# Turning 16-bit tiles: from TensorE transposes to transposing transfers in a two-layer transformer kernel

## The reference

```python
xn = _layernorm(x)
x = x + _L0_attn_ref(xn, ...) + _L0_ffn_ref(xn, w_gating, w_linear)
xn = _layernorm(x)
x = x + _L1_attn_ref(xn, ...) + _L1_ffn_ref(xn, w_gate_up, w_proj)
```

## Time and profile before

| | |
|---|---|
| time, median of 3 runs (lowest, highest) | 600.28 us (598.49, 602.88) |
| the profiled execution: its span, its own time as the profile has it | 601.7 us |
| last sum on VectorE in it | 598.4 us |
| TensorE busy | 562.0 us (93%), 5153 products |
| ScalarE busy | 469.6 us (78%) |
| VectorE busy | 426.6 us (71%) |
| GpSimd busy | 233.6 us (39%) |
| queue 1's packets, share of 16 engines | 24.4% |

### The profile page before, as it was taken

The page is one execution under the profiler, slowest core; times in us unless marked ns, Lnnn a source line. Parts: engine busy times, 40 slices in busy tenths (PEclk is TensorE's granted clock), DMA queues, the critical chain, the costliest instruction groups (busy, mean ns, idle before and its releaser), DMA issues. The chain is left out here.

```text
span 601.7 us, 13300 instructions
## 1 busy us (share of the span) xinstructions
PE 562.0 (93%) x5153; PEld 290.7 (48%) x5153; DVE 426.6 (71%) x909; ACT 469.6 (78%) x607; POOL 233.6 (39%) x302
## 2 busy tenths in 40 slices
...
GB/s 265 303 36 2 36 1 35 36 2 49 6 62 33 33 59 39 27 37 3 19 17 2 64 54 27 89 55 27 54 10 36 45 20 69 17 68 85 94 57 48
DMA packets 150914, 30.40 MB, mean 51 GB/s; under 512 B 133952, under 2 KB 149568, under 8 KB 150848
## 3 DMA queue, kind: packets, MB, share of 16 engines
q1 hardware_dynamic: 150272, 29.19, 24.4%
...
## 5 line engine op out<-in xcount | busy, mean ns | idle before, releaser
L958 ACT ACTIVATE Pt<-psS 128x1024 f32<-128x1024 f32 x288 | 281.7, 1047 | 44.8 <-PE psS L685 25.9
L699 PE MATMUL psV<-Pt,vaug 128*32 128x512 f32 x1152 | 150.3, 611 | 0.3 <-POOL Pt L1645 0.3
L1645 POOL TENSOR_SCALAR_AFFINE_SELECT Pt<-Pt 128x1024 f32<-128x1024 f32 x64 | 71.7, 1145 | 43.8 <-ACT Pt L958 43.8
L685 PE MATMUL psS<-qTf,kTf 32*128 32x512 f16 x576 | 74.9, 390 | 7.3 <-ACT Pt L958 3.7
L685 PEld LDWEIGHTS psS<-qTf,kTf 32*128 32x128 f16 x576 | 20.3, 91 | 82.9 <-ACT Pt L958 48.1
L1695 POOL TENSOR_TENSOR ss<-ss,mhalf 128x1 f32<-128x1 f32 x16 | 9.5, 596 | 111.3 <-DVE ss L1476 111.3
L699 PEld LDWEIGHTS psV<-Pt,vaug 128*32 128x32 f32 x1152 | 25.7, 109 | 41.9 <-issue 35.9
L1016 ACT ACTIVATE stage<-psS 128x1024 f32<-128x1024 f32 x32 | 31.0, 1020 | 8.1 <-PE psS L821 7.9
L1686 POOL TENSOR_TENSOR r<-qk,cos 128x256 f32<-128x256 f32 x16 | 11.9, 744 | 63.9 <-ACT qk L991 58.0
L866 PE MATMUL psB<-wguT,xhs 128*128 128x512 bf16 x108 | 27.8, 380 | 0.0
L1032 ACT ACTIVATE qtmp<-qtmp 128x1024 bf16<-128x1024 f32 x16 | 16.9, 1059 | 12.9 <-PE psA L876 8.4
...
## 6 DMA issues: line engine op xcount, KB each, us to landing
...
G<-qkvscr SPq DMA_DIRECT2D x24, 128.0 KB, 3.7
stage<-in_wg SPq DMA_DIRECT2D x4, 512.0 KB, 8.8
w8g<-qkvscr SPq DMA_DIRECT2D x16, 128.0 KB, 3.8
oscr<-o SPq DMA_DIRECT2D x16, 128.0 KB, 3.3
at<-oscr SPq DMA_DIRECT2D x16, 128.0 KB, 2.0
out<-yout SPq DMA_DIRECT2D x16, 128.0 KB, 2.5
...
```

What stands on the lines that cost most here:

```text
L685: e.matmul(psS[j], kd[32 * j:32 * j + k, h, 128 * at:128 * at + 128], qd[32 * j:32 * j + k, 4 * h:4 * h + 4, :].rearrange("p s n -> p (s n ...
L699: ins = e.matmul(psV[32 * j:32 * j + 32, :], vaug[:, at, j, 32 * h:32 * h + 32], Pt[(4 * Q + j) % NP], start=(kb == 0 and h == 0), stop=(k ...
L958: e.activation(flat(Pt4[:, u % NP:u % NP + 2, :]), flat(psS4[:, j:j + 2, :]), ACT.Exp, scale=scale).then_inc(S["exp"], 1)
L1645: e.affine_select(out=p, in_=p, pattern=[[0, 8], [1, 128]], compare_op=ALU.is_ge, fill=0.0, base=0, channel_multiplier=-1).then_inc(S["mas ...
```

## The change

Three kinds of turns of 16-bit numbers leave TensorE: qxT, the layernorm's xn1T in the first pass, and hxT. Each becomes a transfer of SyncE's queue that turns on its way, from one on-chip buffer into the other (`dma_start_transpose`): kt (2 squares a tile, 64 KB), qt (8, 256 KB), xt (4, 128 KB: the split into 16-bit halves is now made before the turn, by the new stage xs of VectorE) and ht (16, 512 KB). The copies kTc, qTc, xn1Tc and hTc go. 448 transposes of TensorE, 80 fills of the shared banks and 96 operations of VectorE go, 32 of VectorE and 64 transfers come. All other stages keep their order on every engine; the transfers are put between the older ones in SyncE's order. Readers wait for the transfer's semaphore in place of the copy's: qk, qkv1, gu and dn1. Writers wait for it in place of the turn: qh, q0, xs, ssq and hx. ht waits for the dn1 of the tile before.

```diff
     "sp": (
-        "wt.2 wg.2 wg.3 wg.4 wg.5 wt.3 wt.4 wt.5 vw.0 vr.0 vw.1 vr.1 ow.0 at1r.0 vw.2 vr.2 vw.3 ow.1 at1r.1 out.0 "
-        "vr.3 ow.2 at1r.2 vw.4 vr.4 out.1 ow.3 at1r.3 ow.4 at1r.4 vw.5 out.2 vr.5 vw.6 vr.6 vw.7 vr.7 out.3 ow.5 "
-        "vw.8 at1r.5 vr.8 ow.6 out.4 at1r.6 out.5 ow.7 at1r.7 out.6 vw.9 vr.9 ow.8 at1r.8 vw.10 vr.10 ow.9 at1r.9 "
-        "vw.11 ow.10 at1r.10 out.7 out.8 vr.11 vw.12 out.9 vr.12 vw.13 ow.11 vr.13 out.10 at1r.11 vw.14 ow.12 vr.14 "
-        "at1r.12 vw.15 out.11 ow.13 vr.15 at1r.13 ow.14 out.12 at1r.14 ow.15 at1r.15 out.13 out.14 out.15"),
+        "wt.2 wg.2 wg.3 kt.0 qt.0 wg.4 wg.5 kt.1 qt.1 kt.2 qt.2 kt.3 qt.3 wt.3 kt.4 qt.4 kt.5 qt.5 wt.4 xt.0 xt.1 wt.5 "
+        "kt.6 vw.0 vr.0 qt.6 ht.0 kt.7 xt.2 vw.1 vr.1 ow.0 at1r.0 xt.3 qt.7 vw.2 vr.2 ht.1 xt.4 kt.8 vw.3 qt.8 ow.1 "
+        "at1r.1 out.0 vr.3 ow.2 at1r.2 ht.2 kt.9 qt.9 vw.4 vr.4 out.1 ht.3 xt.5 ow.3 at1r.3 kt.10 qt.10 ow.4 ht.4 "
+        "at1r.4 xt.6 kt.11 qt.11 vw.5 out.2 kt.12 qt.12 xt.7 vr.5 ht.5 kt.13 vw.6 vr.6 qt.13 xt.8 vw.7 vr.7 out.3 xt.9 "
+        "ow.5 vw.8 at1r.5 vr.8 kt.14 ow.6 out.4 qt.14 at1r.6 ht.6 out.5 ow.7 ht.7 at1r.7 out.6 vw.9 vr.9 xt.10 ht.8 "
+        "kt.15 ow.8 at1r.8 qt.15 vw.10 xt.11 vr.10 ow.9 at1r.9 ht.9 vw.11 ow.10 at1r.10 out.7 out.8 vr.11 ht.10 xt.12 "
+        "xt.13 vw.12 out.9 vr.12 ht.11 xt.14 vw.13 ow.11 vr.13 out.10 at1r.11 vw.14 xt.15 ht.12 ow.12 vr.14 at1r.12 "
+        "vw.15 out.11 ow.13 vr.15 ht.13 at1r.13 ow.14 out.12 at1r.14 ow.15 ht.14 at1r.15 out.13 ht.15 out.14 out.15"),
...
+            def kt(n):
+                at = n % NT % RING
+                w.wait_ge("q0", n + 1)
+                w.wait_ge("kl", n + 1)
+                w.wait_ge("pv", keys_free(n))
+                e.dma_start_transpose(kT[:, :, 128 * at:128 * at + 128],
+                                      QX[n % len(QX)][:, 32:40, :].rearrange("p h c -> p (h c)")).then_inc(S[f"d_kt{n % 2}"], 16)
+
+            def qt(n):
+                w.wait_ge("qh", n + 1)
+                w.wait_ge("ql", n + 1)
+                if n >= len(qT):
+                    w.wait_ge("qk", 4 * QUAD_END[n - len(qT)])
+                e.dma_start_transpose(qT[n % len(qT)],
+                                      QX[n % len(QX)][:, 0:32, :].rearrange("p h c -> p (h c)")).then_inc(S[f"d_qt{n % 2}"], 16)
+
+            def xt(n):
+                dst = xhs[n % len(xhs)]
+                w.wait_ge("xs", 2 * n + 2)
+                w.wait_ge("qkv1", 2 * (n + 1 - len(xhs)))
+                w.wait_ge("gu", 4 * (n + 1 - len(xhs)))
+                e.dma_start_transpose(dst[:].rearrange("p a (c n) -> p (a c) n", n=128),
+                                      xs_b[n % len(xs_b)]).then_inc(S[f"d_xt{n % 2}"], 16)
+
+            def ht(n):
+                w.wait_ge("hxa", n + 1)
+                w.wait_ge("hx", n + 1)
+                w.wait_ge("dn1", n)
+                w.wait_ge("wsum", 2)
+                e.dma_start_transpose(hT.rearrange("p k s n -> p (k s) n"),
+                                      hx_b.rearrange("p k n -> p (k n)")).then_inc(S["d_ht"], 16)
+
...
-            def qxT(m):
-                n, part = divmod(m, 2)
-                src = QX[n % len(QX)]
-                w.wait_ge("idc", 2)
-                w.wait_ge("q0", n + 1)
-                w.wait_ge("kl", n + 1)
-                if part == 1:
-                    w.wait_ge("qh", n + 1)
-                    w.wait_ge("ql", n + 1)
-                bank = shared("qxT", m)[:].bitcast(F16).rearrange("p (s n) -> p s n", n=128)
-                for at, u in enumerate(range(8) if part else range(8, 10)):
-                    ins = e.transpose(bank[:, at, :], src[:, 4 * u:4 * u + 4, :].rearrange("p r c -> p (r c)"), identh[:])
-                ins.then_inc(S["qxT"], 1)
-
...
                     kd, qd, k = kT, qT[n % len(qT)], 32
-                    w.wait_ge("kTc", n - n % NB + kb + 1)
-                    w.wait_ge("qTc", n + 1)
+                    key = n - n % NB + kb
+                    w.wait_ge(f"d_kt{key % 2}", 16 * (key // 2 + 1))
+                    w.wait_ge(f"d_qt{n % 2}", 16 * (n // 2 + 1))
...
                     src = xhs[n % len(xhs)]
-                    w.wait_ge("xn1Tc", 2 * n + 2)
+                    w.wait_ge(f"d_xt{n % 2}", 16 * (n // 2 + 1))
...
-            def hxT(m):
-                n, pt = divmod(m, 2)
-                w.wait_ge("hx" if pt else "hxa", n + 1)
-                w.wait_ge("idc", 2)
-                bank = shared("hxT", m)[:].bitcast(F16).rearrange("p (s n) -> p s n", n=128)
-                for s in range(8):
-                    ins = e.transpose(bank[:, s, :], hx_b[:, pt, 128 * s:128 * s + 128], identh[:])
-                ins.then_inc(S["hxT"], 1)
-
             def dn1(n):
-                w.wait_ge("hTc", 2 * n + 2)
+                w.wait_ge("d_ht", 16 * (n + 1))
...
             def ssq(n):
                 w.wait_ge("hh", 2 * n + 2)
-                w.wait_ge("hxT", 2 * n)
+                w.wait_ge("d_ht", 16 * n)
                 w.wait_ge("hx", n)
...
-            def kTc(n):
-                at = n % NT % RING
-                bank = psM[filled["qxT", 2 * n] % len(psM)][:].bitcast(F16).rearrange("p (s n) -> p s n", n=128)
-                w.wait_ge("qxT", 2 * n + 1)
-                w.wait_ge("pv", keys_free(n))
-                e.tensor_copy(kT[:, :, 128 * at:128 * at + 128], bank[:, 0:2, :]).then_inc(S["kTc"], 1)
-
-            def qTc(n):
-                bank = psM[filled["qxT", 2 * n + 1] % len(psM)][:].bitcast(F16).rearrange("p (s n) -> p s n", n=128)
-                w.wait_ge("qxT", 2 * n + 2)
-                if n >= len(qT):
-                    w.wait_ge("qk", 4 * QUAD_END[n - len(qT)])
-                e.tensor_copy(qT[n % len(qT)], bank).then_inc(S["qTc"], 1)
...
-                w.wait_ge("xn1T", n + 1 - len(xn1_b))
+                w.wait_ge("xn1T", n + 1 - NT - len(xn1_b))
+                w.wait_ge("xs", min(2 * (n + 1 - len(xn1_b)), 2 * NT))
...
+            def xs(n):
+                src, dst = xn1_b[n % len(xn1_b)], xs_b[n % len(xs_b)]
+                w.wait_ge("xn1", n + 1)
+                w.wait_ge(f"d_xt{n % 2}", 16 * (n // 2))
+                e.tensor_copy(dst[:, 0:256], src[:]).then_inc(S["xs"], 1)
+                w.wait_ge("xs", 2 * n + 1)
+                e.tensor_tensor(dst[:, 256:512], src[:], dst[:, 0:256], ALU.subtract).then_inc(S["xs"], 1)
...
             def hx(n):
                 sn = ss[n % len(ss)]
                 w.wait_ge("hxa", n + 1)
-                w.wait_ge("hxT", 2 * n)
+                w.wait_ge("d_ht", 16 * n)
                 e.scalar_tensor_tensor(hx_b[:, 1, :], h1, sn[:, 2:3], hx_b[:, 0, :], ALU.mult,
                                        ALU.subtract).then_inc(S["hx"], 1)
-
-            def hTc(m):
-                n, pt = divmod(m, 2)
-                bank = psM[filled["hxT", m] % len(psM)][:].bitcast(F16).rearrange("p (s n) -> p s n", n=128)
-                w.wait_ge("hxT", m + 1)
-                w.wait_ge("dn1", n)
-                w.wait_ge("wsum", 2)
-                e.tensor_copy(hT[:, pt, :, :], bank).then_inc(S["hTc"], 1)
...
```

More of the change, by code:

```diff
@@ L170 @@
         "rope.3 gz.0 rs0.6 ql.3 mask.10 mask.11 rope.4 ql.4 xf.0 rope.5 xf.1 rs1.0 rs0.7 ql.5 rs1.1 mask.18 mask.19 "
[14 rows of a table removed]
[17 rows of a table added]
 }
 ROUND = {
[3 rows of a table removed]
[2 rows of a table added]
     "act": "qh QUADS g:0 fh:0 sq:0 th:0 g:1 fh:1 sq:1 th:1 qk1c gTk ex1 tg:0 tg:1 ssq hxa",
[5 rows of a table removed]
[4 rows of a table added]
 }
-PARTS = {"qxT": 2, "fxT": 3, "fTc": 3, "mT": 2, "up": 4, "qkv1": 2, "gT": 2, "gu": 4, "hxT": 2, "sq": 2, "fh": 2, "th": 2,
+PARTS = {"fxT": 3, "fTc": 3, "mT": 2, "up": 4, "qkv1": 2, "gT": 2, "gu": 4, "sq": 2, "fh": 2, "th": 2,
          "tg": 2, "mTc": 2, "g": 2, "ge1": 2, "ge3": 2, "sg": 2,
-         "hh": 2, "hTc": 2, "ge4": 2}
-ROUND2 = {e: r.replace("qxT:0 qxT:1", "fxT:0 fxT:1 fxT:2 rmm mT:0 mT:1").replace(" kl kTc qTc", " fTc:0 fTc:1 fTc:2 rmax mTc:0 mTc:1")
-          .replace(" ql", "").replace(" osum", "") for e, r in ROUND.items()}
+         "hh": 2, "ge4": 2}
 QUAD_STAGES = {"pe": ("qk", "pv"), "act": ("exp",), "pool": ("mask",)}
@@ L215, in one_round @@
     steps = []
-    for word in (ROUND if n < NT else ROUND2)[engine].split():
+    for word in ROUND[engine].split():
         if word == "QUADS":
@@ L236 @@
     "xnT": lambda n: ("xnTc", 2 * n + 2), "qkv": lambda n: ("qkvc", n + 1),
-    "qxT": lambda m: ("qTc" if m % 2 else "kTc", m // 2 + 1), "fxT": lambda m: ("fTc", m - 3 * NT + 1),
+    "fxT": lambda m: ("fTc", m - 3 * NT + 1),
     "mT": lambda m: ("mTc", m - 2 * NT + 1), "obT": lambda n: ("att", 2 * n + 2), "attT": lambda n: ("attTc", n + 1),
     "wo0": lambda n: ("xa", n + 1), "up": lambda m: ("fh" if m % 2 else "g", m // 2 + 1), "down": lambda n: ("yff", n + 1), "flagT": lambda n: ("flag", 1), "wsum": lambda m: ("wmin", m + 1),
```

(16 more changed lines are left out.)

33 lines of the change are left out of this document (18 added, 15 removed), and 245 rows, old and new, of tables (ORDER, ROUND).

## The result

The changed kernel takes 643.77 us, median of 5 runs (642.66 to 648.07), against 600.28 before (median of 5): a ratio of 1.073, 95% interval 1.069 to 1.077, or 43.5 us. The profiled execution's span is 646.3 us instead of 601.7, its last sum ends at 643.7 instead of 598.4. Both profiled executions lie above their medians, the changed kernel's is the slowest of its five, so that the rows differ by 45.3 us where the medians differ by 43.5.

The account below looks back on a forecast made before the run. TensorE and ScalarE were taken to bound the body in turns. Body gain -15.5, start +4, body delays +3 and end +20.3 gave +11.8 on the 600.28 us median: 612 us, range 591 to 645.

Parts of the forecast that it names:

- second rival: The transfer is slow: 643 us if ht takes 10 us, 680 or more at 16; above 628, chance 0.24.
- D: Time for ht (512 KB) to land after its issue: 5.5 us taken, lower bound 3.3, upper 16.
- The work that goes: TensorE: 256 turns of hx, 160 of the cells, 32 of the layernorm, 26.7 us together, 21.2 in the body.
- Of the 21.2 us I take 15.5 as gained, some three quarters: Body, 60 to 540 us: share of TensorE's removed work that shortens the time, bounds 8 and 25 us.
- With small delays of xt I count +3: Body: ssq.7 held 2.8 us by ht.6, plus small delays of xt, together +3 us.
- Held against the times of before, most land well ahead of their reader: Body: of the 64 transfers in SyncE's queue, most land early; one doesn't, the ht that ssq waits for.
- The wait of ssq.7: Body, ScalarE: ssq.7 started at 400.38, but ht.6 lands at 403.2, 2.8 us late, with exponentials queued behind.
- The start: First scores wait for qt: 2.0 us later in tile 0, again 2.0 in tile 2, +4 in all.
- The end: Last 60 us: the loop of dn1, ht and the next ssq, three times uncovered: 4D - 1.7 = 20.3 us.
- Step c: End of dn1.13 to last sum: ht.14, ssq.15 to hx.15, ht.15, dn1: 18.6 us instead of 9.7, 8.9 more.
- Its own signs: Wrong if ht under 4 or above 8, dn1 not waiting, low granted clock at the end, or turns queueing behind one another.

Follow-up runs that it names:

- e1: Kernel before with 352 of its 448 turns left out and no transfer added (values not the reference's): 594.9 us; of 15.2 us less body work 4.3 came in.
- e6: Changed kernel, but the layernorm's turns stay on TensorE (kt, qt and ht by transfer): 619.7 us, ratio to the kernel before 1.027 to 1.037.
- e15: Kernel before with only kt and qt by transfer, kt.0 and qt.0 ahead of loads wt.2, wg.2 and wg.3 in SyncE's order: 601.9 us, ratio 1.001.
- e5: Changed kernel, but hx of the last four tiles (12 to 15) turned by TensorE as before: 623.0 us.
- e8: Kernel before with only hx turned by transfers, all tiles, and a second buffer for hx: 602.9 us, ratio 1.001.
- e12: Changed kernel with ht.13 ahead of vr.15 in SyncE's order, nothing else: 640.7 us, ratio to the kernel before 1.071.

## Why the prediction was wrong

612 us were predicted with a range up to 645; the time lies in the range, at the place of the second rival, but not by its mechanism: D is 3.8, not 10. That is luck. With D = 3.8 and qt's 3.1 the prediction's own sum gives some 604 us, so it was off by 39, and mostly in terms that don't contain D.

- **The work that goes** was right: 448 records of TensorE fewer, 5153 to 4705. But TensorE is busy for 4.0 us less (562.0 to 558.0), not 27: stretches at half clock make the other records longer; how much of it that is wasn't taken apart.
- **"Of the 21.2 us I take 15.5 as gained, some three quarters" is the step that failed first.** e1 gives 28%, so some 6 us, under even the lower bound of 8. I read 98% of cover as "TensorE sets the pace". With 15.2 us less to do in the body it waited more instead (e1), and cutting ScalarE by as much gave only a third as well.
- **"With small delays of xt I count +3"** is the other one. xt costs 11 us alone and some 25 beside the others. "Held against the times of before, most land well ahead of their reader" holds for the cells and for ht in the body; of xt's sixteen, six don't, and at tile 11 the reader followed the old copy's end (465.3) by 0.2 us, which the trace of before shows.
- **The wait of ssq.7**, 2.8 us late in the prediction, was there: ssq.7 waited 2.4 us for ht.6. The exponentials behind it made up for most of it, the first of quad 102 is 0.8 us later against before than that of quad 100 (0.9 in e6).
- **The start**: tile 0 was +2.0 and came to +5.3, as loads ran beside its two transfers (e15); tile 2 was +2.0 on top and came to +1.7, 7.0 in all (55.07 against 48.11). By quad 12 it was 5.0 (78.91 against 73.94).
- **The end**: +20.3 predicted; from qkv1.15 to the last sum 21.6 measured (+23.7 to +45.3), 22 by e5. That ssq waits for ht through the one buffer (e8) and ht.13 for vr.15 (e12) holds. The sizes balanced by luck: D was 3.7 to 5.5 in the four on the path, less than 5.5 in the mean, and the half clock of the last dn1's and products, named and not priced, added 3.2 us in the two dn1 alone. Step c has the right length (18.6 predicted, 18.9 from the end of dn1.13 to the last sum) by another path: wo1.14 and dn1.14 stood behind at1Tc.14, which VectorE has behind ssm.15 and so behind ssq.15, and ht.15 waited for dn1.14, not for hx.15.
- **Its own signs**: two that it gave for being wrong came, ht under 4 and a low granted clock at the end. Tile 11's dn1 started at 576.05 us, 23.0 later than the 553.06 of before, instead of 8 earlier.

Together: start 5.3, body gain -6 at e1's rate, xt some 23 (qkv1.15 stands at +1.0 in e6 and +23.7 in the changed kernel), end 21.6: 44 of 45.3 us. Of xt's 23, 13.6 are TensorE's waits; the rest, half clock behind them among it, wasn't taken apart.
